# Pair products of two samples in one matmul, in two halves around the mix, with the gathers released by the first half

## What is computed

```python
e = stack([tbl_n[ids[:, n]] for n in range(26)], axis=1)      # 512 x 26 x 64, gathered
x = layer_norm(dense @ Wd.T)                                  # 512 x 128
y = layer_norm(einsum('bnd,ed->bne', e, Ws))                  # 512 x 26 x 128
y = layer_norm(einsum('bne,pn->bep', y, Wsi))                 # mix 26 features to 32
T = concatenate([x[:, None, :], swapaxes(y, 1, 2)], axis=1)   # 512 x 33 x 128
Z = einsum('bnd,bmd->bnm', T, T)[:, tril_i, tril_j]           # 528 pair products a sample
z = layer_norm(Z @ Wl.T)[:, :384]                             # 512 x 384
h = relu(concatenate([z, dense]) @ W_top1 + b_top1)
y = relu(h @ W_top2 + b_top2) @ W_top3                        # 512 x 1
```

## Time and profile before

| | us |
|---|---|
| three runs | 209.74, 210.83, 214.5 |
| median | 210.83 |
| profiled execution | 210.07 |
| its span, first to last instruction | 208.2 |
| PE busy | 157.9 (76%) |
| PE weight loads busy | 97.2 (47%) |
| DVE busy | 100.9 (48%) |
| ACT busy | 91.0 (44%) |
| POOL busy | 101.4 (49%) |
| mean granted clock of PE | 0.951 |

### The profile page before, as it was taken

How to read it: one execution, slowest core, us unless ns; L and a number is a source line. 1 busy time by engine, 2 the same in 40 slices (tenths; PEclk the granted TensorE clock), 3 DMA queues, 4 the chain that set the end, 5 groups by cost and what they waited for, 6 DMA issues and landing times.

```text
span 208.2 us, 4120 instructions
## 1 busy us (share of the span) xinstructions
PE 157.9 (76%) x1608; PEld 97.2 (47%) x1608; DVE 100.9 (48%) x197; ACT 91.0 (44%) x227; POOL 101.4 (49%) x113
## 2 busy tenths in 40 slices
PE   0593979688669495888776978497769798979984
PEld 0332635443334353545445764264457445564453
DVE  2463937648177818172736647127354455720041
ACT  2613245454235764253466445025663444442251
POOL 3787575657474755765574747473747200000000
PEclk9998599999999969699999999969996999999999
DMA  5713313144010135211111631110105300052000
GB/s 113 274 25 76 104 41 120 28 158 135 16 33 16 25 117 83 36 25 22 25 19 22 149 62 27 30 19 19 22 19 149 62 3 0 3 135 35 0 3 0
DMA packets 19252, 11.71 MB, mean 56 GB/s; under 512 B 14113, under 2 KB 16673, under 8 KB 19234
## 3 DMA queue, kind: packets, MB, share of 16 engines
q1 hardware_dynamic: 14690, 7.90, 13.8%
q0 software_dynamic: 3328, 3.41, 8.5%
q10 hardware_dynamic: 1216, 0.15, 0.5%
HBM read 9.29 MB, written 2.16 MB: 55 GB/s over the span
## 4 chain that ended last, share of the span: by engine, by line
PE 55%; issue 19%; DVE 7%; ACT 7%; POOL 6%; DMA 4%; another core or an unknown queue 1%; SPq 0%; DVEq 0%; ACTq 0%
PE proj_ps L469 10%; PE mix_ps L436 8%; PE o_ps L484 7%; POOL e_rows L369 6%; PE dots_ps L461 5%; PE quad_ps L447 4%; DMA e_rows<-table_dram,rows_sb 3%; PE turn_ps L428 2%; PE o_ps L488 2%; PE o_ps L399 2%; PE dots_ps L392 2%; DVE x_rstd L861 2%; PE dots_ps L585 1%; PE o_turn_ps L514 1%; PE proj_ps L585 1%
## 5 line engine op out<-in xcount | busy, mean ns | idle before, releaser
L369 POOL DMA_INDIRECT e_rows<-table_dram,rows_sb x104 | 100.5, 967 | 61.0 <-PE dots_ps L461 27.8
L436 PE MATMUL mix_ps<-mixw_sb,e_unit 128*128 128x192 f32 (+4 forms) x128 | 22.9, 324 | 19.4 <-DVE e_unit L906 10.1
L469 PE MATMUL proj_ps<-f_sb,proj_w 128*128 128x512 f32 x64 | 36.7, 660 | 0.2 <-ACT f_sb L666 0.2
L878 DVE TENSOR_TENSOR e_prod<-quad_ps,e_rows 128x384 f32<-128x384 f32 (+1 forms) x16 | 9.5, 591 | 53.7 <-PE quad_ps L447 30.3
L436 PEld LDWEIGHTS mix_ps<-mixw_sb,e_unit 128*128 128x128 f32 x128 | 20.0, 199 | 29.3 <-issue 14.9
L461 PE MATMUL dots_ps<-feats 128*32 128x33 f32 x1024 | 17.0, 199 | 14.1 <-issue 14.1
L461 PEld LDWEIGHTS dots_ps<-feats 128*32 128x32 f32 x1024 | 13.1, 109 | 24.0 <-issue 20.7
L869 DVE TENSOR_REDUCE var_p<-y_sq 128x16 f32<-128x512 f32 x32 | 20.5, 678 | 6.4 <-ACT y_sq L651 6.4
L651 ACT ACTIVATE y_sq<-proj_ps 128x512 f32<-128x512 f32 x32 | 18.9, 590 | 8.6 <-PE proj_ps L469 8.3
L447 PEld LDWEIGHTS quad_ps<-gram,e_cols 128*128 128x128 f32 x104 | 15.9, 224 | 14.1 <-ACT e_cols L659 10.9
L666 ACT COPY f_sb<-mix_ps 64x512 f32<-64x512 f32 x32 | 18.5, 578 | 7.9 <-PE mix_ps L436 5.7
(11 more groups left out here) (132 smaller groups left out, 167.2 us busy)
## 6 DMA issues: line engine op xcount, KB each, us to landing
z_dram<-z_mine SPq DMA_DIRECT2D x4, 512.0 KB, 3.1
e_rows<-table_dram,rows_sb POOLq DMA_INDIRECT x104
w_sb<-w_dram SPq DMA_DIRECT2D x2, 512.0 KB
wl_sb<-wl_dram SPq DMA_DIRECT2D x2, 512.0 KB
w_sb<-w_dram SPq DMA_DIRECT2D x1, 768.0 KB
z_pairs<-z_dram SPq DMA_DIRECT2D x12, 64.0 KB
dense_sb<-dense_t_dram SPq DMA_DIRECT2D x1, 512.0 KB
wl_sb<-wl_dram SPq DMA_DIRECT2D x1, 256.0 KB
```

The lines of the kernel that those rows point to most:

```text
L369: pool.indirect_dma_start(out=e_rows[:, chunk, t, D * ab:D * (ab + 1)], out_offset=None, in_=table, in_offset=bass.IndirectOffsetOnAxis(ap ...
L436: mm = pe.matmul(mix_ps[:, PR * at:PR * (at + number)], e_unit[:, t, :], mixw_sb[:, t, lo:lo + number, :].rearrange("k b p -> k (b p)"), s ...
L469: pe.matmul(proj_ps[:, ab, :], proj_w[:], f_sb[:, q % 2, ab, :], start=True, stop=True).then_inc(projected, 1)
L878: dve.tensor_tensor(e_prod[:, 0:2 * nt, :].rearrange("p a d -> p (a d)"), quad_ps[:, 0:P * nt], e_rows[:, chunk, t0:t0 + nt, :].rearrange( ...
```

## The change

Two samples share one matmul. `feats` holds two samples interleaved, so that 64 columns of weights meet 66 moving columns; the array holds two such pairs beside each other, in strips of 64. Of each 64 x 66 block only the two products of a sample with itself are wanted; the other half is copied but never written out. A slot's dots are now 16 matmuls, in two halves of 8: `dots(i-2, 0)` ahead of the linear part and `mix(i)`, `dots(i-2, 1)` at the end of the round. Both halves use the same columns of `dots_ps`, so the second waits for ACT's copy of the first (`z_half_saved`). ACT's `save_z` is also two copies, each of 264 elements a partition as the one before was; the first stands in `end_round`, ahead of `place_x` and `root_p`, the second at the end of the round.

The gathers of slot s wait for `half_dotted >= s - 3`, the first half of slot s-4, instead of for the whole. `write_z` is four DMAs for the pair products and four for the moments, each from 32 partitions (every second one of 64); the last chunk's are shared by SP and ACT, and ACT's two first `relu_1` of the end now stand behind its wait for these writes. The order of the last round is changed too: `turn(last)` comes first, as in the other rounds, and of `linear(2)` only piece 0 stands ahead of mix. DVE's `norm_p` writes the interleaved layout.

```diff
+WIDE = 2 * (PR + 1)
-        feats = sb("feats", [P, 2, 2 * QB, PR + 2])
-        z_mine = sb("z_mine", [P, CHUNKS, PR + 1, PR])
+        feats = sb("feats", [P, 2, QB, PR + 2, 2])
+        z_mine = sb("z_mine", [P, CHUNKS, 2, PR + 1, PR])
...
+        def write_group(eng, chunk, k, semaphore):
+            mine = slice(k // 2 * HALF + k % 2, k // 2 * HALF + HALF, 2)
+            eng.dma_start(z_dram[chunk, :, PR * k:PR * (k + 1), :].rearrange("b p n -> p b n"),
+                          z_mine[mine, chunk, k % 2, 1:PR + 1, :].rearrange("p (b c) g -> p b (c g)", b=BANDS)
+                          ).then_inc(semaphore, 16)
+
+        def write_moments(eng, chunk, k, semaphore):
+            mine = slice(k // 2 * HALF + k % 2, k // 2 * HALF + HALF, 2)
+            eng.dma_start(s_dram[chunk, PR * k:PR * (k + 1), :], z_mine[mine, chunk, k % 2, 0, :]).then_inc(semaphore, 16)
...
             def write_z(chunk):
                 sp.wait_ge(z_saved, chunk * QUARTERS + QUARTERS)
-                mine = z_mine[:, bass.ds(chunk, 1), :, :]
-                sp.dma_start(z_dram[bass.ds(chunk, 1), :, :, :].rearrange("s b p n -> p (s b) n"),
-                             mine[:, :, 1:PR + 1, :].rearrange("p s (b c) g -> p (s b) (c g)", b=BANDS)).then_inc(z_out, 16)
-                sp.dma_start(s_dram[bass.ds(chunk, 1), :, :].rearrange("s p g -> p (s g)"),
-                             mine[:, :, 0, :].rearrange("p s g -> p (s g)")).then_inc(z_out, 16)
-                sp.wait_ge(z_out, chunk * 32 + 32)
+                for k in range(4):
+                    write_group(sp, chunk, k, z_out)
+                for k in range(4):
+                    write_moments(sp, chunk, k, z_out)
+                sp.wait_ge(z_out, chunk * 16 * 8 + 16 * 8)
...
             def after_round(i):
                 if i >= 2:
-                    pool.wait_ge(dotted, i - 1)
+                    pool.wait_ge(half_dotted, i - 1)
...
-            def dots(s):
+            def dots(s, half):
+                if s == 0 and half == 0:
+                    pe.wait_ge(xsum_saved, 1)
+                if half == 0:
+                    pe.wait_ge(y_ready, 2 * s + 2)
+                    pe.wait_ge(x_placed, s + 1)
+                    wait(pe, z_saved, s)
+                else:
+                    pe.wait_ge(z_half_saved, s + 1)
+                for g in range(QB // 4):
+                    for j in range(2):
+                        f = feats[:, s % 2, QB // 2 * half + 2 * g + j, :, :]
+                        mm = pe.matmul(dots_ps[HALF * j:HALF * (j + 1), WIDE * g:WIDE * (g + 1)],
+                                       f[:, 2:PR + 2, :].rearrange("p c k -> p (c k)"),
+                                       f[:, 0:PR + 1, :].rearrange("p c k -> p (c k)"), start=True, stop=True)
+                mm.then_inc(dotted if half else half_dotted, 1)
...
                 if i >= 1:
                     project(i - 1, 1)
+                if i >= 2:
+                    dots(i - 2, 0)
...
-                    dots(i - 2)
+                    dots(i - 2, 1)
 
             last = SLOTS - 1
+            turn(last)
             project(last - 1, 0)
-            dots(last - 2)
+            quad(last)
             project(last - 1, 1)
-            turn(last)
+            dots(last - 2, 0)
             linear(CHUNKS - 2, range(0, 1))
-            quad(last)
-            linear(CHUNKS - 2, range(1, 3))
             mix(last)
-            linear(CHUNKS - 2, range(3, 4))
+            dots(last - 2, 1)
             project(last, 0)
             project(last, 1)
-            dots(last - 1)
+            linear(CHUNKS - 2, range(1, 3))
+            dots(last - 1, 0)
+            linear(CHUNKS - 2, range(3, 4))
+            dots(last - 1, 1)
             linear(CHUNKS - 2, range(4, KZ + 1))
             top_early(1, 2)
             top_early(1, 3).then_inc(early_done, 1)
-            dots(last)
+            dots(last, 0)
+            dots(last, 1)
...
-            def save_z(s):
+            def save_z(s, half):
                 chunk, q = place(s)
+                act.wait_ge(dotted if half else half_dotted, s + 1)
+                n = QB // 4
+                at = 2 * n * q + n * half
+                act.copy(z_mine[:, chunk, :, :, at:at + n],
+                         dots_ps[:, 0:WIDE * n].rearrange("p (g c k) -> p k c g", c=PR + 1, k=2)
+                         ).then_inc(z_saved if half else z_half_saved, 1)
...
             def end_round(i):
                 square(i, 1)
+                if i >= 1:
+                    save_z(i - 1, 0)
                 place_x(i)
                 root_p(i)
...
             act.wait_ge(z_saved, SLOTS)
-            act.dma_start(s_dram[CHUNKS - 1, :, :], z_mine[:, CHUNKS - 1, 0, :]).then_inc(s_last_out, 16)
+            for k in (2, 3):
+                write_group(act, CHUNKS - 1, k, z_last_out)
+            for k in (2, 3):
+                write_moments(act, CHUNKS - 1, k, s_last_out)
             save_o(CHUNKS - 2)
...
-            for j in range(2):
-                relu_1(j, 0, CHUNKS - 1, 0)
-            act.wait_ge(z_last_out, 16)
+            act.wait_ge(z_last_out, 16 * 4)
             for piece in LAST_BY_ACT:
                 read_piece(act, CHUNKS - 1, z_last, piece, z_last_in[piece[0]])
-            for j in range(2, 4):
+            for j in range(4):
                 relu_1(j, 0, CHUNKS - 1, 0)
...
                 for ab in range(2):
-                    dve.tensor_tensor(feats[:, q % 2, QB * ab:QB * (ab + 1), 2:PR + 2],
+                    dve.tensor_tensor(feats[:, s % 2, QB // 2 * ab:QB // 2 * (ab + 1), 2:PR + 2, :].rearrange("p b q k -> p b k q"),
```

More of the change, by code:

```diff
@@ L256, in tower @@
         wl_summed, z_out = sem("wl_summed"), sem("z_out")
+        half_dotted, z_half_saved = sem("half_dotted"), sem("z_half_saved")
         dense_done, dense_saved, wl_mean_ready, wl_ready, h1_summed, o_saved_dve = (
@@ L334, in _ @@
             sp.wait_ge(z_saved, SLOTS)
-            sp.dma_start(z_dram[last, :, :, :].rearrange("b p n -> p b n"),
-                         z_mine[:, last, 1:PR + 1, :].rearrange("p (b c) g -> p b (c g)", b=BANDS)).then_inc(z_last_out, 16)
-            sp.wait_ge(z_last_out, 16)
+            for k in (0, 1):
+                write_group(sp, last, k, z_last_out)
+            for k in (0, 1):
+                write_moments(sp, last, k, s_last_out)
+            sp.wait_ge(z_last_out, 16 * 4)
             for piece in LAST_BY_SP:
                 read_piece(sp, last, z_last, piece, z_last_in[piece[0]])
-            sp.wait_ge(s_last_out, 16)
+            sp.wait_ge(s_last_out, 16 * 4)
             read_moments(sp, last, s_last_in)
@@ L449, in quad @@
                 mm.then_inc(quad_done, 1)
-            def dots(s):
-                _, q = place(s)
-                if s == 0:
+            def dots(s, half):
+                if s == 0 and half == 0:
                     pe.wait_ge(xsum_saved, 1)
-                pe.wait_ge(y_ready, 2 * s + 2)
-                pe.wait_ge(x_placed, s + 1)
-                wait(pe, z_saved, s)
-                for g in range(2 * QB // 4):
-                    for k in range(4):
-                        f = feats[:, q % 2, 4 * g + k, :]
-                        mm = pe.matmul(dots_ps[PR * k:PR * (k + 1), (PR + 1) * g:(PR + 1) * (g + 1)], f[:, 2:PR + 2],
-                                       f[:, 0:PR + 1], start=True, stop=True)
-                mm.then_inc(dotted, 1)
+                if half == 0:
[11 more added lines that the diff above has]
+                mm.then_inc(dotted if half else half_dotted, 1)
             def project(s, ab):
@@ L682, in place_x @@
                     src = x[:, bass.ds(chunk, 1), :, q, ab, :].rearrange("p s k i -> p (s i) k")
-                    last = act.copy(feats[:, q % 2, QB * ab:QB * (ab + 1), 1].rearrange("p (i k) -> p i k", k=4), src)
+                    last = act.copy(feats[:, s % 2, QB // 2 * ab:QB // 2 * (ab + 1), 1, :].rearrange("p (i j) k -> p i j k", j=2),
+                                    src.rearrange("p i (j k) -> p i j k", k=2))
                 last.then_inc(x_placed, 1)
-            def save_z(s):
+            def save_z(s, half):
                 chunk, q = place(s)
-                act.wait_ge(dotted, s + 1)
-                n = 2 * QB // 4
-                act.copy(z_mine[:, bass.ds(chunk, 1), :, n * q:n * (q + 1)].rearrange("p s c g -> p (s c) g"),
-                         dots_ps[:, 0:(PR + 1) * n].rearrange("p (g c) -> p c g", c=PR + 1)).then_inc(z_saved, 1)
+                act.wait_ge(dotted if half else half_dotted, s + 1)
[4 more added lines that the diff above has]
+                         ).then_inc(z_saved if half else z_half_saved, 1)
             def save_xsum():
@@ L768, in _ @@
                 if i >= 2:
-                    save_z(i - 2)
+                    save_z(i - 2, 1)
             last = SLOTS - 1
+            save_cols(last)
             square(last - 1, 0)
-            save_z(last - 2)
```

(9 more changed lines are left out.)

23 lines of the change are left out of this document (11 added, 12 removed).

## The result

The changed kernel took 240.97 us (240.5 to 245.09, 4 runs), the kernel before beside it 212.67 us: a ratio of 1.143, interval 1.134 to 1.153. It is slower, where 201 us and faster were forecast.

A forecast was written before the change was run, and what follows sets the result against it. It took the closed loop of dots, gathers and turn to bound the kernel. Mix(15) at 158.8 plus an end of 40.8 gave a span of 199.6, plus 1.9 made 201.5, stated as 201 us; 70% range 193 to 206.5, all 192 to 208.

The forecast's parts named there:

- The closed loop: Each round: dots, gathers, turn, round, dots; round 10 is 9.42 us, of which 7.38 us are gathers.
- The trap: Holes inside dots bursts (1.17 us in round 10) taken as the gather wait; nothing counted once gathers come earlier.
- Rival 2: Holes in dots belong to bursts and stay: 0.9 us each over 11 rounds, + 9.7 us, about 210, no change; 13%.
- Release and train: First half releases gathers at turn + 3.4 us; POOL hardly waits, 1.27 us a gather, slot 4 turned at 52.2.
- The half burst: Dots on PE, each half of 16 passes: 0.55 us, plus 0.13 for the change to the next instruction.
- Round 6: One round of PE's loop, paced by the gather train: 7.3 us.
- The path of the pairs: From z_mine through DRAM to `linear`: 10.8 us before, 12.9 with eight writes, reads beginning at 5.7 instead of 3.6.
- The waits of `linear`: PE waits for the chunk's pairs ahead of mix in rounds 7, 11 and 15: 3.3, 2.3 and 3.3 us.
- what the eight writes add: Eight DMA issues instead of two on the path of the pairs: 2.1 us more a chunk.
- the cold clock: Half clock on PE after idle waits, 1.7 us each, two of three waits counted: 3.4 us.
- rival 3: Slower through the path of the pairs: at 16 us the gain is gone, from 17.4 over 2% slower; 7%.
- The end: From mix(15) to the span's end: 35.8 us before, 5.0 more after the change (2 to 8), 40.8.

The follow-up runs named there:

- e2: Kernel before, with the gathers from slot 4 on waiting for quad(i) in mid-round instead of dots(i-2) at its end: 252.21 us.
- e17: Changed kernel, unaltered, run again at another time beside the kernel before (206.74 us): 208.68 us.
- e18: Changed kernel with one z write and one write of the moments a chunk, values in wrong places; second run of this version: 196.39 us.
- e13: Kernel before, with dots of two slots together every second round, one gather release for both, and no wait for the first six slots' gathers: 199.26 us.
- e3: Changed kernel without any wait ahead of the gathers from slot 4 on: 312.09 us.
- e7: Changed kernel with each gather a plain copy of 128 neighbouring rows by POOL, output not the reference's: 211.7 us.
- e9: Kernel before with each gather a plain copy of 128 neighbouring rows by POOL, output not the reference's: 193.7 us.
- e10: Changed kernel with its gathers' lists naming consecutive rows, output not the reference's: 240.94 us.
- e6: Changed kernel with each half doing only 2 of its 8 matmuls, output not the reference's: 223.12 us.

## Why the prediction was wrong

**What bounds before: half right.** The closed loop is real. With plain copies, whose trains last 3.2 instead of 7.4 us, the kernel before takes 193.7 us, against 206.7 with gathers and no standstill. But a part of the loop's time was the standstill: the fastest runs of before took 209.7 to 211.0 us with the condition (medians 212.7 to 216.1) and 202.8 and 203.3 without (206.7 and 207.6). No trace of before without the condition was kept, so that its holes close there is argued from the time alone.

**The trap: this step failed.** "I take these holes for the gather wait in another dress, and count nothing for them once the gathers come earlier." The holes of the earlier trace rows are TensorE held while the train is in flight. They close at the landing because the standstill ends there, not because `turn`'s wait is about to be met; round 8 has none since its burst at 103.66 came when the train was as good as in (issued until 102.65, and 1.15 us more to land). Both readings fit the rows of one kernel; e2 parts them. An earlier release moves a train over more of TensorE's work, so the holes were not to be dropped but multiplied. From the start to mix(15) I had 158.8 us; the trace of after has

```profile
197.26 1.41 PE L449 MATMUL mix_ps<-mixw_sb,e_unit 128*128 128x64 f32 x8
```

at 197.26, 38.5 of the 43.4 us by which its span of 243.0 exceeds the 199.6 of my sum. e17 has it at 162.37, so 34.9 us are the standstill and 3.6 the other terms. Rival 2, with 13%, came nearest: it kept the holes. But it gave them to the bursts as such, not to the gathers in flight, and priced them at the same 0.9 us a burst, + 9.7 us; the price is up to a whole train a round.

**The other steps, read in e17**, where the standstill is absent (sum to a span of 199.6, measured 207.1):

- Release and train: POOL's wait for dots was to fall under 5 us and the last gather to end at 142 to 149. Measured 12.4 us in 5 waits, the longest (3.9 us) in round 6, in which TensorE waits for ScalarE, and the next (3.3 us) behind the pairs of round 11, and 149.95. Turn(4) at 53.0 against 52.3, and turn(5) to turn(6) 6.37 us against "about 7": right.
- The half burst at 0.55 us: the second one at 106.82 is followed by `turn` at 107.44, 0.62 us with the change, where I had 0.68: right. The 231 ns that the profile's page of e17 gives as the mean of a pass overlap with those of its neighbours: 16 passes take 0.69 us.
- Round 6 came to 11.8 us, not 7.3. I had no row for what ScalarE does there:

```profile
68.83 3.63 ACT L732 ACTIVATE wl_sb<-wl_sb,wl_bias,wl_gain 128x512 f32<-128x512 f32 x5
72.49 0.38 ACT L714 COPY z_mine<-dots_ps 128x264 f32<-128x264 f32 x1
72.76 0.48 ACT L681 COPY e_cols<-turn_ps 128x384 f32<-128x384 f32 x1
72.89 2.62 SPq L292 DMA_DIRECT2D z_dram<-z_mine  x4
73.30 1.65 PE L460 MATMUL quad_ps<-gram,e_cols 128*128 128x128 f32 x6 [3.15 <-ACT e_cols L681]
75.56 2.52 SPq L298 DMA_DIRECT2D s_dram<-z_mine  x4
...
80.56 3.48 SPq L286 DMA_DIRECT2D z_pairs<-z_dram  x6
...
84.09 0.51 SPq L301 DMA_DIRECT2D moments<-s_dram  x1
...
86.53 1.10 PE L501 MATMUL o_ps<-wl_sb,z_pairs 128*128 128x512 f32 x2 [2.59 <-DMA moments<-s_dram]
```

- The path of the pairs, in the same rows: z_mine is complete at 72.87, the reads begin 7.7 us later (5.7 predicted), and `linear` starts at 86.53: 13.7 us against 12.9. The eighth issue ends 5.2 us after the first began, where I had 3.2 to its begin; the six reads took 3.5 instead of 4.2. The waits of `linear` came where they were said, 2.6, 2.2 and 3.2 us against 3.3, 2.3 and 3.3.
- But what the eight writes add was mis-sized. With one write the reads start 3.2 us after z_mine:

```profile
72.29 0.38 ACT L711 COPY z_mine<-dots_ps 128x264 f32<-128x264 f32 x1
72.70 0.39 SPq L326 DMA_DIRECT2D z_dram<-z_mine  x1
73.12 0.51 SPq L328 DMA_DIRECT2D s_dram<-z_mine  x1
75.83 4.09 SPq L286 DMA_DIRECT2D z_pairs<-z_dram  x6
```

  so the eight add 4.5 us, not 2.1, and e17 against e18 puts them at 12.3 us: 1.4 in round 7, 3.8 in round 11, 4.1 from turn(15) to mix(15) and 2.8 behind it. The first three are 9.3 us, where the sum had 8.9 for the waits and 3.4 for the cold clock, 12.3. It is rival 3's mechanism, at 13.7 us of path and so below the 16 from which it would have eaten the gain.
- The end was 44.7 us (162.37 to 207.1) instead of 40.8. Of the last chunk, from z_mine to `linear` took 11.1 us, and 8.4 with one write.

The Trainium skill, SBUF — State Buffer, "Door 1: The DMA port swizzle", says that partitions 0 to 63 reach 8 of 16 ports; by its figures the prediction estimated 1 us more a chunk's write. Each transfer of 128 KB landed 2.6 us after its issue by the profile's page of after, where 512 KB took 3.1 before; the time of the path is in the eight issues and the last landing. No run here had the same bytes on other ports, so the rule stays untested.

Without the standstill, then, the forecast would have missed by 7.7 us and the sign by a little: before is 206.7 there, and what the early release and the rest of the change are worth with one write, some 10 us (before 206.7, e18 196.4), is taken back by the writes.

A version that beats both: e13, 199.3 us against 207.6 of before beside it (fastest 198.2 against 203.3) and 208.7 of the changed kernel in e17, all without the standstill. It takes the release off half of the rounds, has no new z layout, and leaves nothing out. With the standstill it wasn't run. e18 would be faster still, but puts values in wrong places.

## What to carry to other kernels

A hole inside a burst whose waits all lie ahead of it is a fact to be explained before it is dropped: look what else is in flight when it opens and closes, and ask what an earlier release will lay over it. When one instruction's result is late, compare the start of its only consumer with its shown end; a matmul shown as ended may not have given its signal. Count the semaphore signals that a trace has against those that it should have: a stretch where they are missing is one where the record and perhaps the run are disturbed. Where a transfer is split, count the issues on its queue up to the last landing, and follow every consumer. And run the kernels to be compared side by side and again at another time: 32 us of the changed kernel's time came and went without an edit.

## What was not expected of the hardware

- In the condition, while POOL's gathers by list are in flight, a narrow burst of TensorE starts some 35 passes and then a few each 0.7 us or more (e2), and results are taken up as much as 5.4 us late (after), 20 us and, of one half burst, 40 us (e3). The quad and turn behind such bursts are late with them; of the signals of other engines that the traces have, none is. Plain copies through the same queue don't do it (e7, e9), consecutive rows in the list don't help (e10), 2 of 8 products still suffer (e6).
- In these stretches 32 to 50% of the semaphore signals of VectorE and ScalarE are missing from the record, and hardly one elsewhere or in e13 to e18. The recording may be part of the cause; no run without it exists.
- It comes and goes on one chip: 240.94 us for the changed kernel's code with other rows in e10, 208.68 us in e17, half an hour later.
- Six gathers cost 7.2 us of POOL and as many plain copies of 32 KB 3.2 us (967 ns against 536 ns each, and no gap of 0.30 us between).
